# An audio tower on one core: quad 0 as a token group of its own, small loads on ScalarE's queue, a new order of steps

## What is computed

```python
h = tok(x)                    # windows of 8 steps: 94 tokens of 64 features
h = h + attn(layernorm(h))    # 8 heads, rank 32
h = h + ffn(layernorm(h))     # 4 heads x 4 experts, causal; gates; 2 small layers; norms
# tok: scores = x . w + b over features; softmax over the 8 steps of a window; weighted sum
# attn: softmax(q k^T / 8) x VO, with q = xQ, k = xK, all tokens to all tokens
# ffn: sx = x hl_w + hl_b; q = sx wq (per expert), k = sx wk, v = sx wv; causal softmax;
#      gate softmax over experts; mixed + sx; layernorm; relu(fx fc1) fc2; + fx; layernorm;
#      each head scaled by a softmax of fout fgate_w
```

## Time and profile before

| | us |
|---|---|
| median of 3 runs | 1000.92 (1000.57 to 1001.37) |
| the profiled execution's own time | 998.95 |
| its span, first to last instruction | 997.2 |
| TensorE, matmul busy | 895.4 (90%) |
| TensorE, weight loads busy | 612.0 (61%) |
| VectorE busy | 803.5 (81%) |
| ScalarE busy | 732.1 (73%) |
| GpSimd busy | 717.3 (72%) |
| mean granted TensorE clock | 0.964 |

### The profile page before, as it was taken

The page is one execution under the profiler, slowest core; times in us unless marked ns, Lnnn a source line. Parts: engine busy times, 40 slices in busy tenths (PEclk is TensorE's granted clock), DMA queues, the critical chain, the costliest instruction groups (busy, mean ns, idle before and its releaser), DMA issues.

```text
span 997.2 us, 39459 instructions
## 1 busy us (share of the span) xinstructions
PE 895.4 (90%) x16312; PEld 612.0 (61%) x16312; DVE 803.5 (81%) x1836; ACT 732.1 (73%) x2743; POOL 717.3 (72%) x1055
## 2 busy tenths in 40 slices
PE   3598999999999999999999999999999999998841
PEld 3265666666676667666676666666676666666630
DVE  3345677888989887989889887989889888888976
ACT  0457786888878887888878887888878888885520
POOL 2333335377887888688888888688878888888893
PEclk9688999999999999999999999999999999999975
DMA  7211111110111111101111111111100000000000
GB/s 197 73 32 40 41 41 41 40 41 12 38 38 44 46 44 45 34 24 44 42 38 45 45 45 45 44 25 36 40 5 14 14 14 14 14 13 13 18 6 19
DMA packets 40932, 36.48 MB, mean 37 GB/s; under 512 B 27313, under 2 KB 30513, under 8 KB 40753
## 3 DMA queue, kind: packets, MB, share of 16 engines
q1 hardware_dynamic: 40656, 33.96, 12.4%
q0 software_dynamic: 96, 0.00, 0.0%
HBM read 25.08 MB, written 3.08 MB: 28 GB/s over the span
## 4 chain that ended last, share of the span: by engine, by line
PE 68%; DVE 22%; ACT 5%; POOL 2%; issue 1%; DMA 1%; POOLq 0%; DVEq 0%
PE psum L778 8%; PE psum L699 7%; PE psum L689 6%; DVE pu L1424 6%; DVE mx L1421 6%; PE psum L727 6%; PE psum L804 5%; PE psum L763 5%; PE psum L681 4%; PE psum L610 4%; PE psum L707 4%; ACT pu L1120 4%; PE psum L623 3%; PE psum L793 3%; PE psum L631 3%; DVE mx L1392 2%
## 5 line engine op out<-in xcount | busy, mean ns | idle before, releaser
L1120 ACT ACTIVATE pu<-psum,mx 128x94 f32<-128x94 f32 x768 | 251.5, 401 | 6.4 <-DVE mx L1392 2.0
L1120 ACT ACTIVATION_READ_ACCUMULATOR pu<-psum,mx 128x1 f32 x768 | 202.4, 269 | 0.0
L1163 ACT ACTIVATE pT<-psum 96x512 f32<-96x512 f32 (+1 forms) x224 | 136.6, 611 | 66.2 <-PE psum L778 65.7
L778 PE MATMUL psum<-ident_w,pu 128*96 128x128 f32 (+1 forms) x896 | 141.5, 281 | 13.0 <-DVE ct L1432 10.8
L508 POOL TENSOR_TENSOR st<-st,neg_half 128x12 f32<-128x12 f32 x64 | 145.7, 2276 | 5.0
L474 POOL TENSOR_TENSOR pu<-pu,pr 128x752 f32<-128x752 f32 x96 | 138.1, 1443 | 13.3 <-DVE pr L1396 13.3
L1392 DVE TENSOR_REDUCE mx<-psum 128x8 f32<-128x752 f32 x96 | 89.4, 939 | 62.8 <-PE psum L689 61.9
L778 PEld LDWEIGHTS psum<-ident_w,pu 128*96 128x96 f32 (+1 forms) x896 | 95.2, 134 | 63.2 <-DVE ct L1432 31.8
L1421 DVE TENSOR_REDUCE mx<-psum 128x16 f32<-128x1536 f32 (+2 forms) x96 | 116.9, 1218 | 11.4 <-PE psum L763 10.8
L1424 DVE TENSOR_TENSOR pu<-psum,mx 128x1536 f32<-128x1536 f32 (+2 forms) x96 | 117.6, 1225 | 3.3
L804 PE MATMUL psum<-gx,ct 128*128 128x84 f32 x768 | 96.5, 275 | 4.3 <-ACT pu L1120 3.6
(11 more groups left out here) (184 smaller groups left out, 2160.6 us busy)
## 6 DMA issues: line engine op xcount, KB each, us to landing
xs<-in_x SPq DMA_DIRECT2D x64, 375.0 KB, 3.7
vb<-va SPq DMA_DIRECT2D x32, 128.0 KB, 2.2
out_h<-ho SPq DMA_DIRECT2D x128, 16.0 KB, 1.4
out_h<-ho SPq DMA_DIRECT2D x128, 7.5 KB, 1.4
vc<-va SPq DMA_DIRECT2D x96, 16.0 KB, 1.9
gx<-in_L_ffn_gate_w SPq DMA_DIRECT2D x16, 0.2 KB
fc<-in_L_ffn_fc_w SPq DMA_DIRECT2D x12, 1.0 KB
fc<-in_L_ffn_fc_b SPq DMA_DIRECT2D x12, 0.1 KB
```

Of the source, the lines that this page charges most:

```text
L778: mm = pe.transpose(psum[0:rows, bank, 128 * e:128 * e + 128], src, ident)
L1120: ins = act.activation(pu[:, j, par, hp, 0:NTOK], psum[:, (low, high)[par], NTOK * hp:NTOK * hp + NTOK], ACT.Exp, bias=mx[:, j, par, hp:hp ...
L1163: act.activation(pT3[j][:, f - (0, 4, 6)[i], :, :, :].rearrange("p e b t -> p (e b t)"), psum[0:rows, bank, :], ACT.Exp).then_inc(p_copied, 1)
```

## The change

Three things are named, and the lists are written anew.

1. Groups of the token layer begin at quads -3, 1, 5, ..., 29. The first holds quad 0 alone (pairs 0 and 1, 24 matmuls), the last quads 29 to 31. The first group's tok_score comes before TensorE waits for the identity and the other constants.
2. The loads of tok_w, tok_b, q_w, k_w, vo_w and 6 of the small loads (hl_w, hl_b, wq, wk, ln_g, fnorm_g) are issued on ScalarE's queue, ahead of its other work. GpSimd clears `tw` and the padding of `xs` first (`padded`).
3. The six count on `ff_first`; make_w and split_w wait for these alone. make_w2 waits for the other 53.
4. Each engine's list has another order, the loop's index runs from -12, and PSUM banks are dealt out anew. The attention's scores use banks 6/7, 1/2 and 6/7, and blocks 1 and 2 are computed at the beginning of the next iteration.

```diff
-FF_LOADS = 16 * (6 * NH + 35)
+FF_LOADS = 16 * (6 * NH + 29)
+FF_FIRST = 16 * 6
...
 # SyncE
-            sp.dma_start(q_w[:, :, :], attn_q.rearrange("h r d -> r h d")).then_inc(attn_loaded, 16)
-            sp.dma_start(k_w[:, :, :], attn_k.rearrange("h r d -> r h d")).then_inc(attn_loaded, 16)
...
-            slow(whl[:, :, 0:NFEAT], hl_w.rearrange("n d h -> d n h"))
...
 # GpSimd
+            pool.memset(tw[:, :], 0.0).then_inc(padded, 1)
+            pool.memset(xs[:, :, NTIME:128 * NCH], 0.0).then_inc(padded, 1)
...
-            pool.dma_start(tw[0:NFEAT, 30:31], tok_w.rearrange("o f -> f o")).then_inc(tok_loaded, 16)
...
 # TensorE
             def tok_score(n, bank):
-                for p in range(2 * GQ):
+                pairs = range(max(0, -2 * n), min(2 * GQ, NPAIR - 2 * n))
+                for p in pairs:
                     slot = (2 * n + p) % NSLOT
                     pe.wait_ge(x_loaded[slot], 16 * ((2 * n + p) // NSLOT) + 16)
...
                 mm.then_inc(tok_scored, 1)
+                if n < 0:
+                    pe.wait_ge(pool_own, 1)
+                    pe.wait_ge(picked, 6)
+                    pe.wait_ge(zeroed, 6)
...
             def make_w(bank):
-                pe.wait_ge(ff_loaded, FF_LOADS)
+                pe.wait_ge(ff_first, FF_FIRST)
...
             def make_w2(bank):
+                pe.wait_ge(ff_loaded, FF_LOADS)
...
 # TensorE's list, in the order of one iteration; index of the quad after the name
+  score(g-1, 1, banks 1,2)   give_outT(g-2)   turn(g+1, 2)   score(g-1, 2, banks 6,7)
+  give_out(g-2)   [tok_score(g+2) where (g+2) % 4 == 1]   mix3(g-4, 0)
+  score3(g-3, 0)  after exp_s(g-1, 1) and add_out(g-2)
+  turn_p3(g-4, 5)   turn_p3(g-4, 4)   turn_c(g-4, 2)  after exp_s(g-1, 2)   turn_c(g-4, 0)
+  [tok_turn(-3) at g = -4]   mix3(g-4, 1)   score3(g-3, 1)   [tok_score(-3) at g = -7]
+  turn_p3(g-3, 1)   turn_p3(g-3, 3)   [make_g at g = -5]   turn(g+1, 1)   turn_x(g)
+  turn_c(g-4, 1)   score3(g-3, 2)   turn_p3(g-3, 0)   front_turn(g-2)   turn(g+1, 0)
+  turn_p3(g-3, 2)   turn_rest(g-6)   project(g, 0)   [make_w at g = 1]   turn_p3(g-3, 6)
+  front_pair(g-2, 1)   layer1(g-6)   front_last(g-2)   pool_x(g+1)   project(g, 1)
+  [tok_turn(g+2)]   front_pair(g-2, 0)   mix(g-1)   score(g, 0, banks 6,7)   layer2(g-6)
+  mix3(g-3, 2)
...
 # ScalarE
+            act.wait_ge(padded, 1)
+            act.dma_start(tw[0:NFEAT, 30:31], tok_w.rearrange("o f -> f o")).then_inc(tok_loaded, 16)
...
+            first(whl[:, :, 0:NFEAT], hl_w.rearrange("n d h -> d n h"))
...
 # VectorE's list, the same way
+  sums(g-1, 1)   soft(g-3, 0)   sums(g-1, 2)   variance(g-7, z)   guard(g-4, 1)   soft(g-3, 1)
+  scale_x(g+1, 1)   head_sum(g-9)   soft(g-3, 2)   scale_x(g+1, 0)   [norm_tok(g+2)]
+  turn_p(g-1, 1)   head_reduce(g-8)   sums_inv(g-4)   turn_p(g-1, 0)   turn_p(g-1, 2)
+  [finish_late(g-9)]   mix_experts(g-5)   mask_hidden(g-6)   gate_shift(g-4)   head_shift(g-8)
+  ln_stats(g+1)   least(g, 0)   mask_second(g-6)   variance(g-5, y)   guard(g-3, 2)
+  centre(g-6)   least(g, 1)   sums(g, 0)   scale_x(g+2, 2)   gate_sum(g-4)   least(g, 2)
+  add_out(g-1)   stats3(g-1)   [soft_tok(g+3)]   guard(g-3, 0)
...
 # GpSimd's list, the same way; G runs 6 ahead of TensorE's g
+  norm_power(G-14, z)   norm_p(G-8, 2)   finish(G-16)   scale, norm_affine(G-14, z)
+  gate_scale(G-11)   head_mul(G-14)   residual(G-13)   norm_power(G-12, y)   gate_weight(G-11)
+  scale(G-12, y)   ln_power(G-6)   norm_affine(G-12, y)   gate_mul(G-11)   power3(G-8)
+  ln_apply(G-6)   norm_p(G-7, 1)   norm_p(G-7, 0)
```

More of the change, by code:

```diff
@@ new lines, in quad @@
+                    if exists(g - 11, NQUAD):
+                        pool.wait_ge(g_inv, 2 * g - 20)
+                        gate_weight(g - 11)
+                    if exists(g - 12, TAIL):
+                        pool.wait_ge(y_rstd, 2 * g - 22)
+                        scale(0, y_mul)
+                    if exists(g - 6, NQUAD):
+                        pool.wait_ge(ln_stat, 2 * g - 10)
+                        ln_power(g - 6)
+                    if exists(g - 12, TAIL):
+                        if exists(g - 12, TAIL):
+                            pool.wait_ge(y_mul, g - 11)
+                        norm_affine(g - 12, 0, fx_made, "j h", fx[:, :, 0:96].rearrange("p h (j c) -> p j h c", c=32))
@@ L600, in _ @@
-            for q in range(-1, 12):
+            for q in range(-3, 12):
                 quad(q)
@@ new lines, in quad @@
+                    if exists(g - 3, NQUAD):
+                        turn_p3(3, 6)
+                    if g + 5 == 0:
+                        make_g(0)
+                    if exists(g + 1, NQUAD):
+                        turn(g + 1, 1, 5)
+                    if exists(g, NQUAD):
+                        turn_x(v % 4, 4)
+                    if exists(g - 4, NQUAD):
+                        pe.wait_ge(c_guarded, 3 * g - 9)
+                        if exists(g - 3, NQUAD):
+                            pe.wait_ge(p_copied, 7 * g - 20)
+                        else:
+                            pe.wait_ge(c_copied, 3 * g - 10)
+                        turn_c(1, 7)
@@ L893, in quad @@
+                    if exists(g - 2, NQUAD):
+                        front_turn(5)
+                    if exists(g + 1, NQUAD):
+                        turn(g + 1, 0, 7)
+                    if exists(g - 3, NQUAD):
+                        turn_p3(2, 6)
                     if exists(g - 6, NQUAD):
@@ new lines, in quad @@
+                    if exists(g - 1, NQUAD):
+                        dve.wait_ge(at_exped, 3 * g)
+                        sums(g - 1, 2)
+                    if g + 3 == 0:
+                        if g + 3 == 0:
+                            dve.wait_ge(tok_exped, 1)
+                        norm_tok(-3)
+                    if exists(g - 7, NQUAD):
+                        dve.wait_ge(z_sq, g - 6)
+                        variance(1, z_eps)
+                    if exists(g - 4, NQUAD):
+                        dve.wait_ge(p_mixed, 3 * g - 9)
+                        guard(v % 2, 1, 4, 5)
@@ L1674, in _ @@
+                    if exists(g + 3, NQUAD) and (g + 3) % 4 == 1:
+                        dve.wait_ge(tok_scored, (g + 6) // 4 + 1)
+                        soft_tok(g + 3, 4)
+                    if exists(g - 3, NQUAD):
+                        dve.wait_ge(p_mixed, 3 * g - 7)
+                        guard((v + 1) % 2, 0, 5)
+            for q in range(-3, 12):
                 quad(q)
```

991 lines of the change are left out of this document (473 added, 518 removed).

## The result

The changed kernel takes 1067.99 us, median of 4 runs (1061.88 to 1072.09), against 1001.14 for the kernel before in the same series: a ratio of 1.066, 95% interval 1.064 to 1.069. It is 67 us slower. The prediction was 992.9 with a range up to 1010. The cause was in none of its parts and in none of its rivals.

What follows compares the result with a forecast made beforehand. TensorE, busy 26.05 of 27.00 us per iteration, was taken to bound the loop. Terms -6.8 (loop), -1.0 (start), -0.9 (last token group), +0.7 (tail) sum to -8.0 us: 992.9 us on the median, range 979 to 1010.

Steps and rivals of the forecast that it cites:

- Part 1: New order in the loop: 0.27 us less per quad, 25 iterations, 6.8 us won; bounds 24 won, 8 lost.
- a new stretch at 0.50 after 101 us: Sign of being wrong: TensorE's clock granted at 0.50 (1.2 GHz) again after 101 us.
- 26.05 us of TensorE's work in any order: Loop: TensorE's busy time per iteration, taken from the old order; with waits an ordinary iteration is 26.85 us.
- The walk to turn_c(2): Loop: TensorE waits at score3(0) from 7.45 to 7.65 us and at turn_c(2) from 9.8 until 10.2.
- the 0.2 at turn_x: Loop: one more TensorE wait of 0.2 us per iteration, ending a chain through GpSimd.
- Part 2: Token groups: quad 0 pooled near 22.6 us, 1.0 won, bounds 2.5 won, 2 lost; last group 0.9 less in the loop.
- part 3: Start, small loads on ScalarE's queue: tok loads land between 4.7 and 11 us; wins nothing beyond Part 2.
- the premise that the x loads pace tok_score(1): Start: tok_score(1) waits for pairs 2 to 9; pair 9 lands between 16.4 and 18.3 us, taken as 17.3.
- Part 4: make_w and split_w wait for 6 loads, not 59, make_w2 for the other 53: zero gain.
- The tail: End of the kernel: finish of quad 30 behind head_reduce of quad 31, 0.7 us lost; bounds 3 won, 4 lost.
- Rival B: Loop: unseen waits as large as those removed; rhythm stays 27.88 us per quad, 999.7 us in total; chance 0.2.
- Rival C: Loop: centre ahead of the second least couples the exponentials to GpSimd's residual; 28.49 us per quad, 1015 us; chance 0.17.

Runs made afterwards that it cites:

- e1_move_first: The changed kernel with SyncE's move_v of quad g+3 ahead of the stores of quad g-3: 1027.37 us, ratio 1.027.
- e8_half_stores: The changed kernel without the third block of tokens of every store, 4 DMAs per quad and not 8: 1026.73 us, ratio 1.025.
- e3_both: The changed kernel with two edits, move_v ahead of the stores and make_g with its copy later (make_g behind tok_score(1)): 1022.07 us, ratio 1.021.
- e6: The kernel before with project ahead of turn_p3(6), apart from the front steps: 1015.17 us, ratio 1.013.
- e12: e3_both with project next to the front steps, ahead of TensorE's wait for fxT, and its ScalarE copies behind exp_p3(6): 1009.17 us, ratio 1.009.
- e2_late_make_g: The changed kernel with make_g behind tok_score(1) in TensorE's list and its copy later in ScalarE's: 1061.68 us, ratio 1.061.
- e7_before_act_queue: The kernel before with the token and attention loads issued on ScalarE's queue, nothing else: 1001.06 us, ratio 0.9988.
- e4_before_store_first: The kernel before with SyncE's stores of quad g-5 ahead of move_v of quad g+1: 1013.18 us, ratio 1.012.
- e10_centre_later: e3_both with centre behind the second least in VectorE's list: 1020.51 us, ratio 1.017.
- e11: e3_both with layer1, then project, directly ahead of both front steps, behind the fxT wait; project's ScalarE copies behind exp_p3(6): 1029.40 us, ratio 1.029.

## Why the prediction was wrong

**The step that failed is one that isn't there.** Part 1 walks TensorE, ScalarE, VectorE and GpSimd, and names for each edit what is queued behind it. SyncE's loop was changed too, and neither the list of changes nor the diff above shows it:

```diff
-                    if exists(g + 1, NQUAD):
-                        sp.wait_ge(f_vc, g + 2)
-                        move_v((v + 1) % 2)
-                    if exists(g - 6, NQUAD):
+                    if exists(g - 3, NQUAD):
...
-                        store(g - 6, v % 2)
+                        store(g - 3, (v + 1) % 2)
+                    if exists(g + 3, NQUAD):
+                        sp.wait_ge(f_vc, g + 4)
+                        move_v((v + 1) % 2)
```

store now stands ahead of move_v, for other quads than before. The prediction has no word on it, neither as a cost, nor as one put at nothing with its cover. Two facts were at hand. In the trace before, SyncE issued the values' moves 0.02 us after they were made, and the stores behind them, at 0.39 to 0.59 us each and 1.83 for the last:

```profile
440.38 0.51 SPq L383 DMA_DIRECT2D vb<-va  x1
...
442.85 0.59 SPq L390 DMA_DIRECT2D out_h<-ho  x1
...
446.20 1.83 SPq L392 DMA_DIRECT2D out_h<-ho  x1
```

These values landed at 444.03, and mix3(2) read them at 474.37, 30 us later. And the output `ho` comes at the end of GpSimd's list for a quad. In the kernel after, seven stores at 0.35 to 0.47 and a last one at 1.90 are 5.1 us with their gaps; with `ho` at 396.55 the moves can't be issued before 401.69 and land 1.8 later, at 405.27. TensorE wanted them at 403.03. In the prediction's walk mix3(2) ends at 2.3 on its clock, with no question of when its values land; that was the step to check. e1_move_first and e8_half_stores show that this is worth 41 us. A part of it comes by the clock. The prediction named a new stretch at 0.50 after 101 us as a sign of being wrong, and the loop of the kernel after has four, of 3.4 us each. This window lies in the first, which follows on 6.7 us in which TensorE was busy for 5.03:

```profile
314.80:318.10 3.30, 3.30 (x34) 1.46 (x28) 2.36 (x5) 0.57 (x4) 1.32 (x1) 0.50 0.47 180
```

The kernel before, e1_move_first and e8_half_stores have none in their loops. At half the speed for 13.7 us that is at most 6.8 of the 41, an estimate.

**The second failed step is the base of the sum, 26.05 us of TensorE's work in any order.** The walk to turn_c(2) came out as predicted: in e3_both score 0 starts at 450.60 and turn_c(2) at 460.89, 10.29 after it, where 10.2 was predicted, with the waits that it named (0.32 at score3(0) for 0.2, and 0.25 at turn_c for 0.4):

```profile
458.52 0.24 PE L750 MATMUL psum<-causB,causA 32*128 32x128 bf16 x4 [0.32 <-ACT pu L1128]
...
460.89 2.02 PE L796 MATMUL psum<-gx,ct 128*128 128x84 f32 x16 [0.25 <-ACT pu L1128]
```

The rest of the iteration was not walked but taken from the 26.05 of the old order. In the new one the same steps cost 0.93 more: project 0.85 for 0.64, layer1 0.63 for 0.43, a turn_p3 ahead of another's wait 0.64 for 0.48, and layer2 0.61 for 0.52. (These four come to 0.66; small differences of other steps, both ways, make up the rest.) A wait of 0.33 at turn_p3(3) was missed, and the 0.2 at turn_x didn't occur. So the sum of idle time (0.8 predicted, 0.9 found) is in part luck. Busy time is the term that was mis-sized: 26.98 where 26.05 stood. With it each quad takes 0.77 us more than before, and 0.77 x 25 = 19 us, of which e6 accounts for 0.41 per quad and e12 takes back 0.36 per quad. The other half isn't isolated, and why a step costs more beside other neighbours stays open.

**Part 2 and 3, the start:** predicted 1.9 won, measured a loss. The direction of the cause was seen ("make_g stands ahead of tok_turn and waits for four more loads"), the size was not. Pair 9 landed at 17.18, as the 17.3 of the prediction, and vo_w at 18.74, where "at 17, no later than pair 9" was put. The real error is the premise that the x loads pace tok_score(1). In e2_late_make_g it starts at 15.62, before pair 9 is there, and runs on to 21.07, 4 us after that load. Behind make_g it could start only at 22.44, since tok_turn, a turn and a scaling had to follow make_g first. A wait in an in-order list delays what could have run, and not only what needs the data. The 1.0 us won from the token groups is shown by no run: with make_g late, quad 0 reaches `hj` at 24.5 to 25.7, in the kernels with the old start at 23.3 to 26.0. The rest of part 3 was right: tokb landed at 9.0, within 4.7 to 11, and the queue by itself is worth 0.2% at most. The Trainium skill's section on issuing engines that the prediction cites in "DMA: Bandwidth & Descriptors" lets it win no more than issue time, and e7_before_act_queue agrees.

**Part 4** was right as far as the traces tell: no wait at make_w. **The tail** was put at 0.7 lost. From the last mix to the end it is 102.0 us in the kernel after against 89.7: 12.3 lost, far outside the bound of 4. SyncE's order makes 8.5 of it, since e1_move_first has 93.5, and e4_before_store_first shows the like in the kernel before. The 3.7 that are left in e3_both (93.4) lie just inside the bound. **Rival B** was the nearest in kind (waits that a walk doesn't see), and its price, the 6.8 us of the gain, was a sixth of what SyncE's order cost. **Rival C**'s mechanism doesn't occur: e10_centre_later.

The sum after the fact, by the spans of the profiled executions (69.5 us longer): 5.7 ahead of the first mix (58.80 against 53.14), 51.5 between the first mix and the last, 12.3 behind it. In e3_both, without SyncE's order and make_g's wait, the three are -0.7, 20.5 and 3.7, and of the 20.5 TensorE's work in 25 iterations is 19. So the two edits take away 6.4 at the start, 31 in the loop and 8.6 in the tail. No version with the new order beats the kernel before; the best form of the new order, e12_project_unwaited, is 0.9% slower.

## What to carry to other kernels

Walk every queue that the change touches, the queues that only issue DMAs first of all: write down for each entry what it waits for, what stands behind it, and who needs that. An output of a late stage placed ahead of an input of an early stage closes a loop through the whole pipeline. It costs nothing where the input has slack (the loop of e4_before_store_first), and 41 us where it has none. When steps are reordered on the engine that bounds the kernel, don't carry over the sum of its busy time: take each step's cost beside its new neighbours, and put a wait in front of the one step that needs it.

## What the runs showed of the hardware that was not expected

- The last of eight store issues in a row took 1.90 us on SyncE, the others 0.35 to 0.47 (after, 399.75). It was 1.83 in the kernel before too (446.20). With four stores fewer, the three `vc` issues behind them took 2.74 us together in place of 1.86 (e8), and in e4_before_store_first the `vb` issue behind eight stores of 0.35 to 0.43 took 1.53 (469.67). A run of DMA issues is not priced by its count alone; why one of them is long is open.
- The same four matmuls of 64x384 (project) took 0.64 to 0.85 us by what stood next to them, though not at a fixed price for each change of tile shape (e6, e11).
- A step that was itself only a small matmul (layer1, 0.6 us) was the cover of a copy on ScalarE; taking it away cost a wait of 0.33 us in each iteration (e11).
- At the start the matmuls of tok_score took a median of 421 ns, later 272 (e2_late_make_g, until 18.6 and from 19.4), at no gap between them. An estimate of a start-up from loop durations is too short.
